# Transformer layer on eight cores: head 0's projections set between layernorm tiles, and a third buffer with a third early layernorm in the feed-forward stage

## What is computed

```python
# _layernorm: (x - mean) / sqrt(var + 1e-5)
def attn(x):
    q = (x @ Wq.T).reshape(b, s, H, DH); k = ...; v = ...
    scores = clip(einsum('bqhd,bkhd->bhqk', q, k) / sqrt(DH), -1024, 1024)
    a = softmax(scores + alibi_causal_mask, axis=-1)
    z = einsum('bhqk,bkhd->bqhd', a, v)
    return einsum('bqhd,ohd->bqo', z, Wo.reshape(d, H, DH))
def ffn(x):
    base = x @ W.T + bias
    top2, idx = top_k(x @ gate_w.T + gate_b, 2); gates = softmax(top2)
    delta = einsum('ner,eor->neo', einsum('nd,erd->ner', x, lora_A), lora_B)
    return base + sum(take(delta, idx) * gates)
x = x + attn(_layernorm(x))
x = x + ffn(_layernorm(x))
```

## Time and profile before

| | us |
|---|---|
| Time, two runs | 4685.03 and 5052.85 (median 4868.94) |
| The profiled execution's own time | 4704.84 |
| Its span, slowest core (core 1) | 4703.3 |
| Spans of the eight cores | 4664.9 to 4703.3 |

### The profile page before, as it was taken

The page is one execution under the profiler, slowest core; times in us unless marked ns, Lnnn a source line. Parts: engine busy times, 40 slices in busy tenths (PEclk is TensorE's granted clock), DMA queues, the critical chain, the costliest instruction groups (busy, mean ns, idle before and its releaser), DMA issues. The chain is left out here.

```text
span 4703.3 us, 65563 instructions; the slowest of 8 cores (4664.9 to 4703.3 us)
## 1 busy us (share of the span) xinstructions
PE 3643.4 (77%) x18452; PEld 1718.1 (37%) x18452; DVE 1917.7 (41%) x5424; ACT 1153.4 (25%) x2606; POOL 110.7 (2%) x210
## 2 busy tenths in 40 slices
PE   2588888888987794777825888888888877948777
PEld 1233434434433341333312334344344333413333
DVE  3435455455455111333334354454554551113333
ACT  4323233233233000111143232332332330001111
POOL 0000000000000001000000000000000000010000
PEclk8687888888878896886756878888888788968888
DMA  4111110110110756111141111101101107561111
GB/s 124 50 23 19 19 23 15 23 19 14 23 19 16 167 159 117 72 72 63 54 130 50 23 19 19 23 15 22 20 15 23 19 14 171 157 117 72 64 72 63
DMA packets 55537, 258.38 MB, mean 55 GB/s; under 512 B 13720, under 2 KB 13984, under 8 KB 34720
## 3 DMA queue, kind: packets, MB, share of 16 engines
q0 software_dynamic: 36464, 119.66, 12.9%
q1 hardware_dynamic: 11824, 84.20, 5.5%
q10 hardware_dynamic: 6912, 50.33, 3.1%
HBM read 273.15 MB, written 67.11 MB: 72 GB/s over the span
## 5 line engine op out<-in xcount | busy, mean ns | idle before, releaser
L841 ACT ACTIVATE prT<-dg,cstt 128x128 bf16<-128x128 f32 (+1 forms) x576 | 217.6, 388 | 1826.5 <-DVE dg L813 1346.1
L802 DVE TENSOR_SCALAR sp<-ps 128x512 f32<-128x512 f32 (+3 forms) x1104 | 631.9, 594 | 14.2 <-PE ps L795 4.6
L795 PE MATMUL ps<-QT,KT 128*128 128x512 bf16 (+3 forms) x1104 | 493.6, 488 | 184.3 <-DVE sp L802 143.4
L1102 PE MATMUL cb<-wf,cT 128*128 128x512 bf16 x2048 | 541.5, 429 | 94.6 <-DMA wf<-wf 83.4
L866 ACT ACTIVATE prT<-sp,cstt 128x128 bf16<-128x128 f32 (+2 forms) x1368 | 581.3, 490 | 16.8 <-DVE sp L802 9.7
L423 PE MATMUL bp<-wo,zTt 128*128 128x512 bf16 x2048 | 467.6, 392 | 74.4 <-DMA wo<-wo 74.4
L639 PE MATMUL pp<-xnT,wv 128*128 128x512 bf16 x2048 | 475.1, 395 | 0.0
L639 PE MATMUL pp<-xnT,wq 128*128 128x512 bf16 x2048 | 447.2, 379 | 0.0
L639 PE MATMUL pp<-xnT,wk 128*128 128x512 bf16 x2048 | 447.2, 379 | 0.0
L733 PE MATMUL pz<-va,prT 128*128 128x129 bf16 x3652 | 389.5, 264 | 26.7 <-ACT prT L866 11.3
L1102 PEld LDWEIGHTS cb<-wf,cT 128*128 128x128 bf16 x2048 | 217.5, 108 | 399.4 <-issue 240.6
(11 more groups left out here) (105 smaller groups left out, 2376.4 us busy)
## 6 DMA issues: line engine op xcount, KB each, us to landing
bx<-x SPq DMA_DIRECT2D x32, 1024.0 KB, 8.0
x2d<-b POOLq DMA_DIRECT2D x32, 1024.0 KB, 9.8
c<-x2d ACTq DMA_DIRECT2D x32, 1024.0 KB, 5.0
out<-co SPq DMA_DIRECT2D x32, 1024.0 KB, 3.9
prT<-x ACTq DMA_DIRECT2D x16, 1024.0 KB, 5.8
prT<-x SPq DMA_DIRECT2D x16, 1024.0 KB, 5.8
wv<-wv POOLq DMA_DIRECT2D x32, 512.0 KB, 6.1
wq<-wq POOLq DMA_DIRECT2D x32, 512.0 KB, 6.0
```

Source lines behind the costliest of these rows:

```text
L795: lambda e, c=c, q0=q0, n=n, bank=bank: e.matmul(psc[bank][:, 0:n], KT[:, c * 128:(c + 1) * 128], QT[:, q0 * 128: q0 * 128 + n], start=Tru ...
L802: lambda e, n=n, bank=bank, buf=buf: e.tensor_scalar(spanb[buf][:, 0:n], psc[bank][:, 0:n], 1024.0, -1024.0, ALU.min, ALU.max),
L841: soff=soff: e.activation(probsT[:, pslot:pslot + min(ncols, 128)], diagb[:, soff:soff + min(ncols, 128)] if ncols == 64 else diagb[:, 0:128],
L1102: lambda e, bi=bi, dc=dc, og=og, bk=bk: e.matmul(b["pb"][bk][:, :], b["xnT2"][bi][:, dc * 128:(dc + 1) * 128], b["wfT"][:, dc * D + og * 5 ...
```

## The change

Three things change.

1. `proj` becomes `proj_unit`, one unit of 16 matmuls and its evacuation. For heads 1 to 15 the order of units stays. For head 0 the twelve units of v, q and k come in a mixed order from the list `sched`, and `ln_plan` says which layernorm tiles stand ahead of each: four ahead of the first unit, two ahead of each of the next six, none ahead of the last five.
2. The buffers `x2b`, `xnb`, the small columns `cc` and the semaphores `cxl` of the feed-forward block go from two to three, indexed by `i % 3`. The load of tile i then waits for the last addition of tile i-3, and also for the store of its data (`b_stores`).
3. In block B a third early layernorm is appended, for tile 2, behind tile 2's additions and store.

```diff
+    if h == 0:
+        sched = [("v", 0), ("q", 0), ("v", 1), ("k", 0), ("v", 2),
+                 ("q", 1), ("v", 3), ("k", 1), ("q", 2), ("k", 2),
+                 ("q", 3), ("k", 3)]
+        ln_plan = {0: (0, 1, 2, 3), 1: (4, 5), 2: (6, 7), 3: (8, 9),
+                   4: (10, 11), 5: (12, 13), 6: (14, 15)}
+        for ui, (kind, tg) in enumerate(sched):
+            for i in ln_plan.get(ui, ()):
+                ln_cb(i)
+            w_sb, dst, wi, scale, mm_l, ev_l = P3[kind]
+            proj_unit(w_sb, dst, wi, tg, ui % 2, scale, mm_l, ev_l)
+            if tg == 3 and h + 1 < NH:
+                wd = {"v": dram["wv"], "q": dram["wq"], "k": dram["wk"]}[kind]
+                prefetch(wi, wd, w_sb, mm_l[3])
...
-                if i == 1:
-                    for t0 in range(2):
+                if i in (1, 2):
+                    for t0 in ((0, 1) if i == 1 else (2,)):
                         pld = pg.op("scalar",
                                     lambda e, t0=t0: e.dma_start(
                                         cx2b[t0][:, :], x2_d.ap()[t0]),
                                     inc=sem["cxl"][t0], amt=16,
-                                    waits=[(sem["dsb"][t0], store_tok[t0])])
+                                    waits=[(sem["dsb"][t0 % 2],
+                                            b_stores[t0])])
...
             ld = pg.op("scalar",
-                       lambda e, i=i, bi=bi: e.dma_start(
-                           b["x2b"][bi][:, :], x2_d.ap()[i]),
-                       inc=sem["cxl"][bi], amt=16,
-                       waits=[(s_dve, apply_tok[bi]), (s_dve, ev_out[bi])])
+                       lambda e, i=i, bi3=bi3: e.dma_start(
+                           b["x2b"][bi3][:, :], x2_d.ap()[i]),
+                       inc=sem["cxl"][bi3], amt=16,
+                       waits=[(s_dve, apply_tok[bi3]),
+                              (s_dve, ev_out[bi3]),
+                              (sem["dsb"][i % 2], b_stores[i])])
```

More of the change, by code:

```diff
@@ L168, in build_program @@
             cxl=[Ctr(es.enter_context(nc.semaphore(f"s_cxl{i}")))
-                 for i in range(2)],
+                 for i in range(3)],
             wpre=[Ctr(es.enter_context(nc.semaphore(f"s_wpre{i}")))
@@ L378, in _build_seq @@
         cx2b = [bces.enter_context(nc.sbuf_tensor(f"c2{s}{i}", [P, D], F32))
[L379 removed]
+                for i in range(3)]
         cxnb = [bces.enter_context(
[L381 to L382 removed]
+            nc.sbuf_tensor(f"cn{s}{i}", [P, D], BF16)) for i in range(3)]
+        ccc = bces.enter_context(nc.sbuf_tensor(f"cc{s}", [P, 24], F32))
         with ExitStack() as bes:
@@ L537, in _build_seq @@
             _plan_ffn(pg, s, cb, sb, sem, wf_tok, lora_tok, x2_d, out_d,
-                      prefix)
+                      prefix, b_stores)
+            for _p in range(3):
+                pg.wait("scalar", sem["cxl"][_p], sem["cxl"][_p].n)
             for _p in range(2):
-                pg.wait("scalar", sem["cxl"][_p], sem["cxl"][_p].n)
                 pg.wait("sync", sem["dob"][_p], sem["dob"][_p].n)
@@ L620, in _plan_head @@
     off = {c: prow[c][0] for c in range(NT)}
[L622 to L663, removed]
@@ new lines, in proj_unit @@
+    def proj_unit(w_sb, dst, wi, tg, bk, scale, mm_last, ev):
+        for dc in range(NDC):
+            w = []
+            if h == 0:
+                w.append((s_dve, st["xnT_cp"][4 * tg + 3][dc // 4]))
+            if dc == 0:
+                if tg == 0:
+                    w.append((sem["wpre"][wi], wtok[h][wi]))
+                w.append((s_dve, st["proj_evac"][bk]))
+            tk = pg.op(
+                "tensor",
+                lambda e, dc=dc, tg=tg, bk=bk, w_sb=w_sb: e.matmul(
+                    ppb[bk][:, :],
+                    w_sb[:, dc * DH:(dc + 1) * DH],
+                    xnT[:, dc * SEQL + tg * 512:
+                        dc * SEQL + (tg + 1) * 512],
+                    start=(dc == 0), stop=(dc == NDC - 1)),
+                inc=(s_pe if dc == NDC - 1 else None), waits=w)
+            if dc == NDC - 1:
+                mm_last[tg] = tk
+        if scale is None:
+            ev[tg] = pg.op("vector",
+                           lambda e, tg=tg, bk=bk, dst=dst: e.tensor_copy(
+                               dst[:, tg * 512:(tg + 1) * 512],
+                               ppb[bk][:, :]),
+                           inc=s_dve, waits=[(s_pe, mm_last[tg])])
+        else:
+            ev[tg] = pg.op("vector",
+                           lambda e, tg=tg, bk=bk, dst=dst, scale=scale:
+                           e.tensor_scalar(
+                               dst[:, tg * 512:(tg + 1) * 512],
+                               ppb[bk][:, :], scale, None, ALU.mult),
+                           inc=s_dve, waits=[(s_pe, mm_last[tg])])
+        st["proj_evac"][bk] = ev[tg]
@@ L671, in prefetch @@
             inc=sem["wpre"][wi], amt=16, waits=[(s_pe, gate_tok)])
[L673 to L681, removed]
+    v_mm, v_ev = [0] * 4, [0] * 4
+    q_mm, q_ev = [0] * 4, [0] * 4
+    k_mm, k_ev = [0] * 4, [0] * 4
+    P3 = {"v": (b["wv"], vTs, 2, None, v_mm, v_ev),
+          "q": (b["wq"], QT, 0, 1.0 / math.sqrt(DH), q_mm, q_ev),
+          "k": (b["wk"], KT, 1, None, k_mm, k_ev)}
+    if h == 0:
+        sched = [("v", 0), ("q", 0), ("v", 1), ("k", 0), ("v", 2),
[11 more added lines that the diff above has]
+                prefetch(wi, wd, w_sb, mm_l[3])
+    else:
+        for kind in ("v", "q", "k"):
+            w_sb, dst, wi, scale, mm_l, ev_l = P3[kind]
+            for tg in range(4):
+                proj_unit(w_sb, dst, wi, tg, tg % 2, scale, mm_l, ev_l)
+            if h + 1 < NH:
+                wd = {"v": dram["wv"], "q": dram["wq"], "k": dram["wk"]}[kind]
+                prefetch(wi, wd, w_sb, mm_l[3])
     last_tr = 0
@@ L913, in _plan_ffn @@
         bi = i % 2
+        bi3 = i % 3
         if i < len(prefix):
```

37 lines of the change are left out of this document (19 added, 18 removed).

## The result

The changed kernel takes 4725.65 us (median of 27 runs), the kernel before 4698.04 us (median of 26). The ratio is 1.0058, with a 95% interval of 1.0036 to 1.0080. By the 2% bound this is no change, but the interval lies clear of 1: the kernel became slower by some 27 us. The fastest runs say the same, 4709.74 against 4681.60. The profiled execution took 4754.53 us. In it the cores 0 to 3 spanned 4729.4 to 4753.0 us at a mean clock of 0.797 to 0.802, and the cores 4 to 7 spanned 4691.6 to 4706.0 at 0.807 to 0.810.

A forecast was written before the change was run, and what follows sets the result against it. The prediction took TensorE's idle time as what counts, with its layernorm waits set by VectorE's order. Terms +10.2 + 21.2 - 10.3 = +21.1 us on 4704.84, less 16.6 for a slow stretch, gave 4709 us; range 4680 to 4760.

The forecast's parts named there:

- the sum: Whole kernel: +10.2 for head 0, +21.2 for block B, -10.3 for the feed-forward block, together +21.1 us.
- within 2%, +0.4%: Whole kernel: 4709 us counts as no change, since about 2% is what a measurement can tell; chance 0.91.
- the stall of block B: Block B, tile 5: TensorE waits 9.0 and 8.8 us for VectorE's additions of tile 3; with slow restarts +21.2 us.
- Part 1: Head 0: moved units q0, k0, q1 take turns with layernorm tiles, 5.15 us each against 3.45; +10.2 us in two sequences.
- Part 2: Feed-forward block: third buffer costed at nothing, as VectorE's order holds the layernorm; 26 waits of 4.4 us stay from tile 3.
- Rival 1: Feed-forward block: the third buffer removes all 28 layernorm gaps, 5.1 us each, -143 in place of -10.3; 4577 us; chance 3%.
- Part 3: Third early layernorm: saves 10.3 us in the feed-forward block, adds 21.2 us of waiting and restart in block B.
- The restart: Block B, behind the gap: TensorE restarts at the lower clock level, +1.7 us a sequence.
- more than 6 us a sequence: Feed-forward block: shortening beyond this would show the prediction wrong; at most 5.93 us, taken as 5.1, was expected per sequence.
- rival 2: Head 0: q0, k0, q1 run hidden under the layernorm chain, -20.7 us in place of +10.2; 4678 us; chance 8%.
- rival 3: Block B: no stall, VectorE done with tile 3 by 1639.4, 9.0 us earlier than worked out; 4688 us; chance 15%.
- rival 4: From block B's gap through C: TensorE's lower clock spreads over some 1200 us, +133 us; 4842 us; chance 6%.

## Why the prediction was right and wrong

**What was wrong.** Two steps failed. One is the last, from the sum to the number. I called the case "within 2%, +0.4%" and took 2% for what a measurement can tell. The comparison resolves 0.22% to either side, and the change is a slowdown that lies clear of it. The sum said +21 us, slower, by mechanisms each with its sign, and I set the result down as no change and as 4709, a number below the median of the two runs that were shown. Against the measured medians the number is 17 us short. The base for it, 4704.84 less 16.6, was a good one: the fastest runs of before are at 4682 and many near 4687.

The other is a term. The mechanisms held, but the sum of 21.1 us is 7.0 short of the 28.1 between the fastest runs, and the largest miss is the stall of block B: 21.2 taken, 24.5 measured. Of the rest some 3 us have no cause shown; the third buffer, taken at nothing, may cost as much, which is not clear of the noise. That 4725.9, the sum before 16.6 was taken off, stands beside the measured median of 4725.65 is chance: from the fastest run of before the sum leads to 4702.7, where 4709.74 was measured.

**Part 1, the projections.** Right in mechanism and nearly in size: +10.2 worked out, 10.8 between the fastest runs with and without it, and 5.8 us a sequence in head 0 on cores 4 to 7 against 5.1. The difference has a source. I priced the moved units by the waits for v0, v1 and v2, 4.54 in the mean; the moved ones showed 5.02 to 5.44 us, since more of their matmuls ran at the lower level of the clock (q0 took 6.07 us for its 16, where rows 2 had 5.10). The unit of rows 2 is read by its pace alone: its first matmuls start 0.43 us apart, while the profile gives a granted clock of 1.00 for core 1 from 56 to 62 us. At core 6's q0 pace and clock agree.

**Part 2, the third buffer.** Right: 28 waits, 124.4 us together, with the buffer alone, and a ratio of 1.0010. Rival 1 had the gap right and its cause wrong. The two kernels with the early layernorm settle it: with VectorE's order changed, two buffers are no worse than three. The Trainium skill, "Perfetto Trace Analysis", section Optimization Strategy, says of a repeated gap that it can mean too few buffers; here the trace does not agree, since the 28 gaps stayed with three buffers and went with the order.

**Part 3, block B.** The mechanism was right and the size too small: 21.2 taken, 24.5 by the late third layernorm. I had 8.9 us of wait a sequence; on the eight cores tile 5 waits 10.3 on average. In the first sequence the store took 8.8 to 10.3 us until the load could go, 9.5 in the mean (8.77 taken), and the load with its passes 9.4 (9.28 taken). The cover was smaller too: from the store of tile 2 until TensorE was done with tile 4 it was 13.6 to 15.2 us, 14.3 in the mean, and 14.8 taken. Rows 5 are of a core that had 0.9 us of room between tile 2's additions and tile 4's matmuls; a core without it, like core 6, waits there first (1.21 us). That small wait is not a cost of the change, since four cores had it before. The restart cost 2.0 us: tile 5 took 14.9 to 16.2 us from its first matmul to its first addition, 15.6 in the mean of the eight cores, against 13.57 where a tile began behind a short wait (before, core 2, 1622.54 to 1636.11); 1.7 was taken. On core 6 the granted clock is 0.50 for the first 2 us. Together 21.0 less 0.7 of before and twice 2.0 is 24.3.

In the feed-forward block I took 10.3 us of saving and 5.93 a sequence at most. The fastest runs give 9.9 (4695.10 without the third layernorm, 4685.24 with it placed late), the lengths of tiles 1 to 3 give 6.1 a sequence, 12.1 in both. I had named more than 6 us a sequence as a sign of being wrong; the tiles just reach it, and which of the two figures is nearer stays open.

**The sum.** 10.8 + 14.6 = 25.4 us of the 28.1 between the fastest runs are accounted for. The medians of the comparable runs give 10.6 and 14.5. Some 3 us are left, of the size of what the third buffer may cost (2.0 by the fastest runs), and stay open.

**Rivals 2, 3 and 4.** The units were not hidden as the kernel stood (rival 2); they were once the evacuation stood behind L600. There was no lack of a stall (rival 3). The lower clock did not spread after the stall (rival 4): core 6, with a stall of 11.98 us, has a mean clock of 0.810, as high as the cores before, and in the fastest run all eight cores have 0.808 to 0.811. Cores 0 to 3 are lower in the profiled execution (0.797 to 0.802), but core 1 had its slow stretch at 200 us, long before the stall, and a granted clock of 0.97 from 1655 to 1850 us, right behind it.

## What to carry to other kernels

Where an engine works a fixed list, read what stands behind a waiting instruction before adding a buffer or moving work: a unit set between two chains hides nothing if its evacuation stands ahead of the next chain, and costs next to nothing (0.43 us instead of 5.15) if it stands where the chain waits anyway. A gap that repeats at every tile is first a question of where the next tile's first operations stand. An operation that needs a store's data belongs well behind the store: two tiles were enough here, none cost 24.5 us.

## What the runs showed of the hardware that was not expected

In the profiled execution of the changed kernel core 1 ran a wholly dense stretch of head 0 at a granted clock of 0.81, between the two levels, while core 6 ran its own at 1.00. The two windows (us, busy PE, PEld, DVE, ACT, POOL with counts, clock, DMA share, GB/s), core 1 first and core 6 in the second fence:

```profile
197.00:218.00 21.00, 21.00 (x82) 8.70 (x80) 3.46 (x5) 0.00 (x0) 1.06 (x2) 0.81 0.26 41
```

```profile
190.00:207.00 17.00, 17.00 (x80) 7.70 (x79) 3.46 (x5) 0.00 (x0) 1.06 (x2) 1.00 0.27 42
```

A unit of 16 matmuls takes 4.20 us on the one, 262 ns a matmul, and 3.45 on the other, 216 ns. In the stretch of rows 10 core 1 took 9.64 us for 32 matmuls with `wf` (from 2135.22 us), 301 ns each. These are two slower paces of the same dense work. They came on pairs of cores: from 200 to 205 us cores 0 and 1 had 0.81 and the other six 1.00; in the profile of the kernel with the late third layernorm cores 0, 1, 4 and 5 had 0.81 from 200 to 206 us and the other four 1.00; and the mean of 0.69 in rows 10's stretch was on cores 0 and 1 alone. All eight cores doing dense matmuls is not enough to bring them on: in block B before, from 1660 to 1770 us, all eight ran at 1.00. What does was not tried.
